# Expert weights chosen by a register, in one copy of the tile's code

## The reference

```
gate_scores = xf @ gate_w.T
top1 = jnp.argmax(gate_probs, axis=-1)
one_hot = jax.nn.one_hot(top1, N_ROUTING, dtype=xf.dtype)
masked = xf[None, :, :] * one_hot.T[:, :, None]
h = jax.nn.relu(jnp.einsum('end,edh->enh', masked, w1) + b1[:, None, :])
expert_out = jnp.einsum('enh,ehd->end', h, w2) + b2[:, None, :]
routing_output = expert_out.sum(axis=0)
shared = jax.nn.relu(xf @ sw1 + sb1) @ sw2 + sb2
return (routing_output + shared).reshape(B, S, D)
```

## Time and profile before

| | us |
|---|---|
| median of 3 runs | 1998.26 (1997.72 to 2003.76) |
| the profiled execution, its own time | 1997.06 |
| its span, first to last instruction | 1995.3 |
| PE busy | 1884.6 (94%) |
| PE weight loads busy | 1202.5 (60%) |
| DVE, ACT, POOL busy | 887.6, 848.3, 520.6 |

### The profile page before, as it was taken

How to read it: one execution, slowest core, us unless ns; L and a number is a source line. 1 busy time by engine, 2 the same in 40 slices (tenths; PEclk the granted TensorE clock), 3 DMA queues, 4 the chain that set the end, 5 groups by cost and what they waited for, 6 DMA issues and landing times. The chain is left out here.

```text
span 1995.3 us, 32828 instructions
## 1 busy us (share of the span) xinstructions
PE 1884.6 (94%) x11964; PEld 1202.5 (60%) x11965; DVE 887.6 (44%) x1668; ACT 848.3 (43%) x1506; POOL 520.6 (26%) x635
## 2 busy tenths in 40 slices
PE   8889999999899999999999999999989798989997
PEld 6344444444566666666666665666656565656664
DVE  6989888889343333333333333222222222222222
ACT  4644444444334444444444443334334243333333
POOL 1068888887100001000001002111211111212111
PEclk9999999999999999999999999999999899999998
DMA  9145555554822222222222526111110111111100
GB/s 322 65 141 172 173 170 171 170 166 152 301 76 75 93 88 95 94 74 74 82 97 91 193 97 251 35 33 34 43 35 30 31 34 31 33 34 44 43 18 15
DMA packets 123641, 198.20 MB, mean 99 GB/s; under 512 B 20208, under 2 KB 61680, under 8 KB 123120
## 3 DMA queue, kind: packets, MB, share of 16 engines
q1 hardware_dynamic: 115584, 171.01, 25.7%
q0 software_dynamic: 7920, 25.17, 3.9%
HBM read 137.95 MB, written 58.98 MB: 99 GB/s over the span
## 5 line engine op out<-in xcount | busy, mean ns | idle before, releaser
L1024 DVE TENSOR_TENSOR room_a<-room_a 128x256 f16<-128x256 f32 (+1 forms) x528 | 233.6, 443 | 935.9 <-ACT room_a L1011 931.9
L978 PE MATMUL pH<-room_a,room_f 128*128 128x256 f16 x4608 | 572.4, 275 | 34.7 <-issue 29.4
L990 PE MATMUL pY<-room_f,room_a 128*128 128x512 f16 x2304 | 559.6, 380 | 4.6 <-DVE room_a L1024 4.6
L978 PEld LDWEIGHTS pH<-room_a,room_f 128*128 128x128 f16 x4608 | 454.8, 99 | 165.3 <-issue 39.5
L1009 ACT ACTIVATE room_a<-pH,e_bsel,sc 128x256 f32<-128x256 f32 (+1 forms) x272 | 151.6, 557 | 454.3 <-PE pH L978 432.4
L990 PEld LDWEIGHTS pY<-room_f,room_a 128*128 128x128 f16 x2304 | 225.6, 98 | 197.4 <-DVE room_a L1024 4.9
L1009 ACT ACTIVATE room_a<-pH,b1s,sc 128x256 f32<-128x256 f32 x256 | 144.2, 563 | 365.2 <-PE pH L978 364.5
L978 PE MATMUL pH<-room_a,room_v 128*128 128x256 f16 (+1 forms) x1728 | 202.7, 269 | 14.8 <-issue 14.5
L1171 POOL TENSOR_TENSOR room_a<-room_a,s_brow 128x512 f32<-128x512 f32 x32 | 42.4, 1344 | 617.6 <-DVE room_a L1032 617.6
L978 PEld LDWEIGHTS pH<-room_a,room_v 128*128 128x128 f16 x1728 | 162.7, 99 | 64.8 <-issue 19.1
L990 PE MATMUL pY<-room_v,room_a 128*128 128x512 f16 x816 | 198.1, 379 | 0.0
(11 more groups left out here) (191 smaller groups left out, 1785.5 us busy)
## 6 DMA issues: line engine op xcount, KB each, us to landing
room_b<-in_w SPq DMA_DIRECT2D x64, 256.0 KB, 4.3
s_er<-in_w SPq DMA_DIRECT2D x32, 512.0 KB, 6.5
rows_room<-in_x SPq DMA_DIRECT2D x32, 256.0 KB, 4.5
room_a<-in_sw SPq DMA_DIRECT2D x32, 256.0 KB, 4.8
room_b<-in_x SPq DMA_DIRECT2D x32, 256.0 KB, 2.8
s_split<-room_a SPq DMA_DIRECT2D x64, 128.0 KB, 4.2
x_scratch<-room_b SPq DMA_DIRECT2D x32, 256.0 KB, 3.0
z_scratch<-room_b SPq DMA_DIRECT2D x32, 256.0 KB, 3.4
```

Source lines behind the costliest of these rows:

```text
L978: mm = q.matmul(self.pH[j % 2][:, 0:rows], w[:, k, j * P:(j + 1) * P], zt[:, u, k, 0:rows], start=(n == 0), stop=(n == 3 * KC - 1))
L990: mm = q.matmul(self.pY[u][r][:, :], h[:, j % self.HR, r * P:(r + 1) * P], w[:, j, :], start=(j == 0 and n == 0), stop=(j == HC - 1 and n ...
L1024: q.tensor_tensor(self.hl[:, j % self.HR, 0:rows], self.hf[:, j % self.HR, 0:rows], self.hh[:, j % self.HR, 0:rows], ALU.subtract).then_in ...
```

## The change

The two rooms become one tensor, `room_w`, with the room as its second dimension; `room_f` and `room_v` are now names for its halves. The If goes. For each tile PE's sequencer loads two numbers from SBUF: the half of the room to use (`flags`, now `is0`, so that 1 means `room_v`), and the count that the semaphore must have (`needs`, 64 for expert 0 and 128 for expert 1). Both loads raise one semaphore, `w_in`, the first set to 64 and the second to 128; SP issues the second set only when the first is there. The tile's code stands once and finds its weights by an address in a register.

```
--- before.py
+++ after.py
-        room_f = sb("room_f", [P, 4, 8192], F16)
-        room_v = sb("room_v", [P, 4, 8192], F16)
+        room_w = sb("room_w", [P, 2, 4, 8192], F16)
+        room_f, room_v = room_w[:, 0, :, :], room_w[:, 1, :, :]
...
+def chosen_set(room_w, half):
+
+    def view(i, n):
+        return room_w[:, bass.ds(half, 1), i, :].rearrange("p h (k n) -> p (h k) n", n=n)
+
+    return tuple(view(i, n) for i, n in enumerate((HID, HID, DM, DM)))
...
-                        load_set(nc, sp, wB, e1_d, e2_d, 0, w0_in)
+                        load_set(nc, sp, wB, e1_d, e2_d, 0, w_in)
...
                 sp.wait_ge(snet.S["e_out"], 64 * TILES)
-                load_set(nc, sp, wA, e1_d, e2_d, 1, S["w1_in"])
+                sp.wait_ge(w_in, 64)
+                load_set(nc, sp, wA, e1_d, e2_d, 1, w_in)
...
-                def tile(q, g, u, weights, loaded):
-                    q.wait_ge(loaded, 64)
+                def by_expert(q, g, u):
+                    t = bass.ds(net.tile(g, u), 1)
+                    half = q.value_load(flags[0:1, t], min_val=0, max_val=1)
+                    need = q.value_load(needs[0:1, t], min_val=64, max_val=128)
+                    q.wait_ge(w_in, 64)
+                    q.wait_ge(w_in, need)
+                    weights = chosen_set(room_w, half)
                     for j in range(HC + net.LAG):
...
-                def by_expert(q, g, u):
-                    e = q.value_load(flags[0:1, bass.ds(net.tile(g, u), 1)], min_val=0, max_val=1)
-                    with q.If(e == 0):
-                        tile(q, g, u, wB, w0_in)
-                    with q.Else():
-                        tile(q, g, u, wA, S["w1_in"])
-
...
-                pe.wait_ge(S["flags"], 1)
+                pe.wait_ge(S["flags"], 2)
...
-                dve.tensor_copy(flags[:, :], is1[:, :]).then_inc(S["flags"], 1)
+                dve.tensor_copy(flags[:, :], is0[:, :]).then_inc(S["flags"], 1)
+                dve.tensor_scalar(needs[:, :], is1[:, :], 64.0, 64.0, ALU.mult, ALU.add).then_inc(S["flags"], 1)
```

More of the change, by code:

```diff
@@ L892, in xattn_ffn @@
             iz = sb("e_iz", [P, Net.N, Net.R], I32, f)
-            w0_in = f.enter_context(nc.semaphore("w0_in"))
+            w_in = f.enter_context(nc.semaphore("e_w_in"))
             pH = [ps(f"pH{n}", [P, 512], f) for n in range(2)]
@@ L899, in xattn_ffn @@
             snet.S["e_out"] = f.enter_context(nc.semaphore("s_e_out"))
-            room = (sb, ps, sc, wA, wB, cacc, order, inv, is1, is0, eh, el, iz, w0_in, snet, enet, stored, first_in)
+            room = (sb, ps, sc, wA, wB, room_w, cacc, order, inv, is1, is0, eh, el, iz, w_in, snet, enet, stored, first_in)
             shared_net(nc, room, x1_d, z_d, res_d, (s1_d, s2_d), (e1_d, e2_d), units, w1, w2, sb2, net_scales,
@@ L1056, in shared_net @@
 def shared_net(nc, room, x1_d, z_d, res_d, split_s, split_e, units, w1, w2, sb2, net_scales, consts, cols):
-    sb, ps, sc, wA, wB, cacc, order, inv, is1, is0, eh, el, iz, w0_in, net, enet, stored, first_in = room
+    sb, ps, sc, wA, wB, _, cacc, order, inv, is1, is0, eh, el, iz, w_in, net, enet, stored, first_in = room
     ones, upper, lane, row_id, starts, amw, b1e, b1e_s, b1s, expert1 = consts
@@ L1419, in experts @@
 def experts(nc, room, z_d, res_d, out, split_e, b2, consts):
-    sb, ps, sc, wA, wB, cacc, order, inv, is1, is0, eh, el, iz, w0_in, snet, net, _, _ = room
+    sb, ps, sc, wA, wB, room_w, cacc, order, inv, is1, is0, eh, el, iz, w_in, snet, net, _, _ = room
     ones, b1e_s = consts
@@ L1425, in experts @@
         N, S, step, R = net.N, net.S, net.step, net.R
-        for n in ("w1_in", "b2_in", "flags", "idle", "idle_row", "pick_r", "pick_o", "bias", "sel0", "sel", "b2s", "bias0"):
+        for n in ("b2_in", "flags", "idle", "idle_row", "pick_r", "pick_o", "bias", "sel0", "sel", "b2s", "bias0"):
             S[n] = f.enter_context(nc.semaphore("e_" + n))
@@ L1429, in experts @@
         flags = sb("e_flags", [P, SLOT_TILES], I32, f)
+        needs = sb("e_needs", [P, SLOT_TILES], I32, f)
         ir = sb("e_ir", [P, N, R], I32, f)
```

## The result

The changed kernel takes **1951.5 us** in the median of four times: 1949.5, 1950.04, 1952.96 and a disturbed one of 4015.61 us, without which the median is 1950.04 us. That stands against 1998.1 us (1997.72 to 2003.76, four times) for the one before on the same chip: a ratio, without the disturbed time, of **0.9757, 95% interval 0.974 to 0.9775**. Run again beside two variants, in a later set of runs, it took 1949.39 us, 0.976 (0.9747 to 0.9773) of the kernel before. The forecast was 1949.

A forecast was written before the change was run, and what follows sets the result against it. TensorE was taken to bound the kernel, idling in the expert phase on code fetches behind far jumps. Terms -55.7 + 5.6 + 0.1 + 1.0 = -49.0 us gave 1948.1 us, 1949 as median; range 1943 to 1966.

The forecast's parts named there:

- The bound and the size of what goes: Expert phase: TensorE waits on jumps to code that must be fetched; 55.7 us of excess goes with the second copy.
- short gaps cost no clock: Tile starts: after a short gap (1.44 us) the 36 matmuls take 4.12 us, so the clock does not fall.
- The loop of some 1570 instructions stays resident: Expert loop on TensorE: its branch, four times taken, costs 0.2 us in the sequencer's lead and PE nothing.
- Register operations at 0: Before weight address changes, 2720 in 17 tiles: hidden, 0 us (at most 354); +1 us in the half tile.
- The split of the tokens becomes last: Tile starts: splitting the next z ends last, 0.37 us for each of 15 starts, 5.6 us; bounds 0 to 16 us.
- Waits on the weights and the joined rooms at 0: Waits moved to register operations, SP's wait for the first set, and two rooms made one: no cost.
- The sum: Whole profiled execution: -55.7 + 5.6 + 0.1 + 1.0 = -49.0 us, giving a forecast median of 1949 us.
- The loop still fetches: Rival, chance 0.18: the expert loop's four back edges fetch code, 13 us plus up to 9 for the clock; 1965 us.
- The sequencer: Rival, chance 0.05: register operations make the sequencer the bound in expert steps, +136 us at 0.26 us each; 2085 us.
- Only the long gaps go: Rival, chance 0.05: gaps of about 1.4 us at ordinary tile starts stay, 21 us; gain 34 us, 1964 us.

The follow-up runs named there:

- near_if: Changed kernel, but an If on the flag picks only the wait (64 or 128) and the count's load goes; products stand once: 1949.43 us.
- if_reg: Changed kernel with the If put back around two copies of the tile, both register-addressed and waiting for the tile's count: 2029.07 us.
- fixed: Changed kernel, but every tile uses the first expert's weights at fixed addresses, without register operations ahead of the matmuls: 1948.68 us.
- best: Changed kernel with the next tile's transposes and token split, and its flag and count loads, all moved to step 13 of the tile before: 1945.5 us.
- early: Changed kernel with the next tile's token transposes and split moved to step 13 of 16, loads left in place: 1951.24 us, then 1946.16 us.
- all128: Changed kernel without the per-tile count: every tile waits for both weight sets (128): 1979.85 us.
- pf_all: Changed kernel with all tiles on the first expert's weights at fixed addresses, plus a spare-register operation before every product; loop of 1823 instructions: 1979.57 us.
- p_all: Changed kernel plus an operation on a spare register in front of every expert product; loop of 1823 instructions: 1993.23 us.
- e_loop4: Changed kernel with TensorE's loop body doubled to four tiles in 3131 instructions, one branch back instead of four: 1954.99 us.

## Why the prediction was right, step by step

**The bound and the size of what goes** (55.7 us of excess over 16 tiles without a gap). Right. From the first start to that of the half tile are now 725.4 - 36.64 = 688.8 us, against the 681.7 worked out as free of gaps: an excess of 7.1 where 55.7 were, 48.6 us gone. near_if shows that it was the distance of the jump, if_reg that the change of addressing alone brings none of it. The 9 us of slow clock came back too: the windows at the 15 starts behind the first all show 1.00, where the one of the earlier trace rows showed 0.63, and the longest gap at a start is now 0.3 us. No run kept the gaps while holding the clock. The sentence that short gaps cost no clock holds for the gaps of 1.0 to 1.7 us that it was read from; in if_reg, six of 2.3 to 3.0 us did.

**The loop of some 1570 instructions stays resident.** Right, and in part by luck of size: 1823 does not. The argument from rows could only say "between 1240 and 2470". The rival took the two-page window from the Trainium skill, "Runtime: NRT & Kernel Launch", section "Instruction fetch mechanics"; the traces contradict it for TensorE: a target 1567 instructions back, six pages of 256, is reached in 0.21 us with no packet (changed kernel). The same section's 2048 instructions for TensorE are nearer, but a loop of 1823 is fetched anew on every turn, so that the room for a loop is smaller than that figure.

**Register operations at 0.** Nearly right: 4.0 us in all (fixed). The steps of the full tiles are free, as worked out. The 1.8 us in the gaps I had counted, as the operations behind the split. What I left out are the first 36 products of a tile, where nothing covers the operations: 0.09 us a start, 1.4 us. The half tile's 0.8 us (I had 1.0) lies at its start too, and not in its steps, where I had put it.

**The split of the tokens becomes last, 0.37 us x 15 = 5.6 us.** The place is right (five waits for L1017), and so is the size: 5.0 us, by best. The loads are hidden as I had it, with 1.6 us to spare and not 1, as the records shown under early have it. My bound said that they would cost when their cover is gone, and early is that case: it gets 3.0 of the 5.0 us. Of the 7.1 us of excess that are left, best keeps 2.1. The first 36 products, read from fixed, are 1.4 us of these; the rest wasn't tried apart.

**Waits on the weights and the joined rooms at 0.** Right; all128 shows that the counts are needed for it.

**The sum.** -49.0 forecast, -48.1 in the phase (725.4 - 773.4). The profiled run then had 4.0 us more ahead of the phase, by the chance of its start and not by the change: a second profile has 0.4. Medians: -46.6 us (-48.1 without the disturbed time) and, beside the variants, -49.1 us. The forecast of 1949 for the median is as close as it is partly by chance, since the start of the phase alone moves by up to 6 us.

**The rivals.** *The loop still fetches* (1965): pf_all has four gaps of 2.9 to 3.4 us, where I had priced 3.2; so the price was right and the condition not met. Of the up to 9 us for the clock added to it, pf_all shows about 1 us in two of four gaps, and p_all 0.7 to 0.9 us in each of four. *The sequencer* (2085): never near, 0.137 us a product at most, where 0.23 was needed. *Only the long gaps go* (1964): no; starts lie 43.0 us apart, the starts with short gaps gained 1.2 us each too (44.2 before).

## What to carry to other kernels

Look at the sequencer's branch records before anything else when TensorE waits for "issue": if branches take microseconds and the instruction queue moves packets inside a loop, the code of the loop is too long for the store, or laid out with jumps over copies. One body whose operands come from a register removes both, and inside the tiles of this kernel the register operations were free as long as a step's products times 0.14 us stayed under the step's time and the loop's body stayed below the length that is refetched (between 1567 and 1823 instructions here, with two for each matmul). Then read the choice and prepare the next tile's operands some steps ahead of the tile, both together: moving one of them took away the cover of the other; and when one body replaces two, give it the wait of the case at hand, not the larger of both.

## What the runs showed of the hardware

- TensorE's instruction store, seen through loops: 1247 and 1567 instructions come back in 0.2 us; 1823, 2470 and 3131 (and 3122 in if_reg) take 3.3 to 4.8 us for the branch. Packets on the instruction queue are 16 KB; the changed kernel draws 27 for the 6784 instructions from the first expert tile to the end, one for about 250. A loop that lies on 8 pages draws 9 each turn (pf_all), one on 13 pages 14 (e_loop4).
- A branch over one or two instructions takes 0.06 to 0.21 us, taken or not (near_if).
- The sequencer passes a product with a register operation in front of it in 0.12 (plain) to 0.137 us (plain and fused mixed), seen where matmuls are short enough to uncover it.
- Idle gaps of 2.3 to 3.4 us sometimes lower the granted clock and sometimes don't: 0.71 and 5.79 us for 36 products in pf_all after one of 3.31 us, but 1.00 and 4.77 us after one of 3.38 us; 0.70 and 5.77 us in if_reg after one of 2.34 us, but 4.24 us after 2.83 us in e_loop4. The four of 3.0 to 3.7 us in p_all all lower it. What tells these apart stays open.
- TensorE's sequencer stands at a wait of an operation and goes on right behind it: the last low half is ready at 1309.63 us in the changed kernel, and the operations behind that wait start at 1309.7, the load at 1309.9.
- The start of the experts' phase varies by 6 us between kernels whose code before it is the same; early, 3 us better in the phase, seemed worth nothing in its first set of runs, and the late start of its profiled execution fits that.
